# The context pass writes into the tiles of self attention, and three loads and stores are cut or moved

## The reference

```python
x = x + tanh(g_xattn[0]) * router_attention(layernorm(x), f, f, ctx, Wq, Wk, Wv, Wlq, Wlk, Wo, bo)
x = x + tanh(g_ffn[0])   * quantised_ffn(layernorm(x), w1, conv_w, conv_b, w2)
x = x + tanh(g_xattn[1]) * attention(layernorm(x), ctx, ctx, Wq, bq, Wk, bk, Wv, bv, Wo, bo)
x = x + tanh(g_ffn[1])   * recurrence(layernorm(x), wf, uf, bf, wi, ui, bi, wc, uc, bc, wo, uo, bo, in_c)
```

## Time and profile before

| | us |
|---|---|
| median of three runs | 2679.94 (2677.76 to 2680.05) |
| the profiled execution, its own time | 2680.58 |
| its span, first to last instruction | 2678.8 |
| PE busy | 2359.8 (88% of the span) |
| DVE, ACT, POOL busy | 1442.3, 1061.0, 603.7 |
| `ctx` ends, `att` starts (its first POOL instruction) | 113.6 |
| `att` ends, `ffn` starts | 1061.6 |
| `ffn` ends, `xat` starts | 1608.1 |
| `xat` ends, `rec` starts | 2020.9 |

### The profile page before, as it was taken

How to read it: one execution, slowest core, us unless ns; L and a number is a source line. 1 busy time by engine, 2 the same in 40 slices (tenths; PEclk the granted TensorE clock), 3 DMA queues, 4 the chain that set the end, 5 groups by cost and what they waited for, 6 DMA issues and landing times. The chain is left out here.

```text
span 2678.8 us, 40715 instructions
## 1 busy us (share of the span) xinstructions
PE 2359.8 (88%) x16307; PEld 1553.5 (58%) x16348; DVE 1442.3 (54%) x1746; ACT 1061.0 (40%) x1227; POOL 603.7 (23%) x204
## 2 busy tenths in 40 slices
PE   7359999999999986798999877999978999999989
PEld 6235555555555543344445425766656788888867
DVE  4345565665655554477677766787753222222235
ACT  3324444444544532344455543444432222222222
POOL 0004545554646544000000002233220000000000
PEclk9679999999999988899999997999988999999999
DMA  8711010110110011111111112222213000000036
GB/s 243 182 34 38 12 46 18 38 46 10 46 41 15 25 44 63 60 44 52 47 47 53 43 63 61 70 84 71 99 68 114 32 31 31 31 31 31 16 143 219
DMA packets 102030, 163.73 MB, mean 61 GB/s; under 512 B 17012, under 2 KB 39540, under 8 KB 99118
## 3 DMA queue, kind: packets, MB, share of 16 engines
q1 hardware_dynamic: 95934, 150.82, 17.5%
q10 hardware_dynamic: 6000, 11.54, 1.1%
HBM read 112.63 MB, written 49.71 MB: 61 GB/s over the span
## 5 line engine op out<-in xcount | busy, mean ns | idle before, releaser
L1047 DVE TENSOR_REDUCE att_mx<-att_sn 128x2 f32<-128x1024 f32 x256 | 313.7, 1226 | 170.4 <-PE att_sn L854 168.1
L959 ACT ACTIVATE att_num<-att_st 128x2048 f32<-128x2048 f32 x128 | 240.5, 1879 | 147.1 <-PE att_st L842 90.3
L766 POOL TENSOR_TENSOR att_es<-att_es,att_num 128x2048 f32<-128x2048 f32 x64 | 293.0, 4578 | 15.6 <-ACT att_num L959 9.4
L762 POOL TENSOR_TENSOR att_es<-att_num 128x2048 f32<-128x2048 f32 x32 | 146.0, 4561 | 388.9 <-PE att_pj L824 343.8
L2405 ACT ACTIVATE rec_ga<-rec_g,rec_bg 128x512 f32<-128x512 f32 x84 | 57.1, 687 | 307.8 <-PE rec_g L2306 307.8
L2306 PE MATMUL rec_g<-weights_a_h,row_weights_h 128*128 128x512 f32 x384 | 153.5, 400 | 13.6 <-ACT rec_ga L2405 11.1
L854 PE MATMUL att_sn<-att_kh,att_qh 32*128 32x512 f32 x512 | 128.5, 498 | 38.2 <-DVE att_mx L1047 38.2
L2306 PE MATMUL rec_g<-weights_a_l,row_weights_h 128*128 128x512 f32 x384 | 152.2, 396 | 0.0
L2306 PE MATMUL rec_g<-weights_a_h,row_weights_l 128*128 128x512 f32 x384 | 151.9, 396 | 0.0
L1360 PE MATMUL ffn_h<-ffn_xqt,ffn_w 128*128 128x512 bf16 x486 | 119.4, 389 | 28.1 <-DVE ffn_hs L1615 21.2
L1615 DVE TENSOR_TENSOR ffn_hs<-ffn_h,ffn_fb 128x1024 f32<-128x1024 f32 x64 | 78.1, 1220 | 118.6 <-PE ffn_h L1360 109.2
(11 more groups left out here) (383 smaller groups left out, 5690.1 us busy)
## 6 DMA issues: line engine op xcount, KB each, us to landing
rows<-in_x SPq DMA_DIRECT2D x16, 1024.0 KB, 5.4
rows<-x SPq DMA_DIRECT2D x16, 1024.0 KB, 5.2
rows_b<-in_fside_BxSxS SPq DMA_DIRECT2D x8, 1024.0 KB, 7.6
heads<-att_o SPq DMA_DIRECT2D x32, 256.0 KB, 2.3
weights_b_l<-heads SPq DMA_DIRECT2D x8, 1024.0 KB, 5.4
x<-ffn_xr SPq DMA_DIRECT2D x32, 256.0 KB, 2.0
xat_xr<-x SPq DMA_DIRECT2D x8, 1024.0 KB, 5.3
x<-xat_xr SPq DMA_DIRECT2D x8, 1024.0 KB, 4.3
```

The costliest lines, as they stand in the source:

```text
L762: pool.tensor_tensor(ES[:], E[0][:], E[1][:], ALU.add).then_inc(s_sum, 1)
L766: pool.tensor_tensor(ES[:], ES[:], E[k][:], ALU.add).then_inc(s_sum, 1)
L959: act.activation(E[k][:], st_ps[:], ACT.Exp, scale=SCALE).then_inc(s_exp, 1)
L1047: dve.tensor_reduce(MX[c % 2][:, m // 2, 2 * DH * (m % 2):2 * DH * (m % 2) + DH + 1:DH], sn_ps[:], AX, ALU.max, negate=True).then_inc(s_ma ...
```

## The change

1. Self attention's tiles are allocated around `ctx`: it gets `weights_a` (WA), `weights_b` (WB), the row tiles `rows` (XROW) and `rows_b` (FROW), and Wq, Wk, x, f. It keeps Wlq and Wlk in WA and WB, then Wv in WA, then the next pass's Wk in WB and Wq in WA. The stages of Wv, the next Wk and the next Wq are XROW, FROW and the tile of the masked `rq`. Batch 0 of x and f is loaded in `ctx` too, and the layer norm of x is done there. `att` starts with these at hand, loads only Wv and the routers, and makes Wv's halves after the task `("k", 1)` of `AHEAD`.
2. In `ctx` the order of PE's list is new (`v` behind all `e`, two `k` before `e 6`), the routines of ACT and DVE are hung on other entries, and the keys lie in the memory of RK. The keys are stored by one DMA with 2464 numbers per partition; the DRAM layout is (P, C, B, G), so that a load of keys in `xat` has rows of 77 numbers where it had rows of 154.
3. `ffn` loads the first matrix in four column parts, the heads of batch 1 after the first; the second matrix is loaded after the rows of batch 1. `hidden(0, 0)` waits for the first part alone, and `low_half(1)` comes behind `scaled(0, 1)`.
4. `xat`: nothing waits for the tables but the first `q`; the tanh is made after `AHEAD`, and its users wait there. The last batch's rows are stored tile by tile, 4 x 256 KB.

```diff
-    ORDER = [("rq", 0), ("rk", 0), ("rq", 1), ("rk", 1), ("v", 0), ("e", 0), ("e", 1),
...
-             ("rq", 4), ("rk", 4), ("v", 3), ("e", 6), ("e", 7), ("v", 4)] + [("k", i) for i in range(2 * C)]
+    ORDER = [("rq", 0), ("rk", 0), ("rq", 1), ("rk", 1), ("e", 0), ("rq", 2), ("rk", 2), ("e", 1), ("e", 2),
+             ("rq", 3), ("rk", 3), ("e", 3), ("rq", 4), ("rk", 4), ("e", 4), ("e", 5), ("k", 0), ("k", 1),
+             ("e", 6), ("e", 7)] + [("v", t) for t in range(NT)] + [("k", i) for i in range(2, 2 * C)]
...
+        NAMES = ("lq", "lk", "k", "v", "next_k", "next_q")
...
+        stage = {"lq": quarter(0), "lk": quarter(1), "k": quarter(2), "v": XROW[:], "next_k": FROW[:],
+                 "next_q": RQS[:, 0:C, :]}
...
+            for n, dram in (("lq", Wlq), ("lk", Wlk), ("k", Wk), ("v", Wv), ("next_k", next_wk)):
+                sp.dma_start(stage[n], kxn(dram)).then_inc(s_w[n], 16)
...
+            load_second(3)
+            for group, n in enumerate(("lq", "lk", "k")):
+                sp.wait_ge(s_lo, step(n))
+                load_second(group)
...
+            for b in range(5):
+                store_routers(b)
+            sp.wait_ge(s_lo, step("v"))
+            sp.dma_start(XROW[:], first(x)).then_inc(s_row, 16)
+            sp.wait_ge(s_lo, step("next_k"))
+            sp.dma_start(FROW[:], first(f)).then_inc(s_frow, 16)
+            for b in range(5, B):
+                store_routers(b)
+            sp.wait_ge(made["e"], B)
+            sp.dma_start(stage["next_q"], kxn(next_wq)).then_inc(s_w["next_q"], 16)
+            sp.wait_ge(s_sign, 4)
+            sp.dma_start(t1_s, TERNARY[0]).then_inc(s_store, 16)
+            for t in range(NT):
                 store_values(t)
...
-            for b in range(B):
-                sp.dma_start(k1_s[b].rearrange("p (c g) -> p c g", c=C), K[:, :, b * G:b * G + G]).then_inc(s_store, 16)
+            sp.wait_ge(taken["k"], 2 * C)
+            sp.dma_start(k1_s, RKS[:, 0:C * N]).then_inc(s_store, 16)
             sp.wait_ge(s_sign, 8)
             sp.dma_start(t2_s, TERNARY[1]).then_inc(s_store, 16)
...
-                if (kind, i) == ("v", 2):
+                if (kind, i) == ("rq", 3):
                     total(0)
-            total(1)
+                if (kind, i) == ("v", 4):
+                    total(1)
...
+            TODO = {("rq", 0): [("high", "k")], ("rk", 4): [("high", "v"), ("high", "next_k")],
+                    ("e", 4): [("sign", 0, 0)], ("e", 5): [("sign", 0, 1)], ("e", 7): [("sign", 0, 2), ("sign", 0, 3)],
+                    ("v", 4): [("high", "next_q")], ("k", 2): [("sign", 1, 0)], ("k", 3): [("sign", 1, 1)],
+                    ("k", 4): [("sign", 1, 2)], ("k", 5): [("sign", 1, 3)], ("k", 7): [("rows",)]}
...
+            TODO = {("rk", 0): lambda: low("k"), ("rk", 1): lambda: sums(0, 0), ("e", 0): lambda: sums(0, 1),
+                    ("rk", 2): lambda: sums(0, 2), ("e", 1): lambda: sums(0, 3), ("e", 2): lambda: mean(0),
+                    ("rk", 3): lambda: whole(0, 0), ("e", 3): lambda: whole(0, 1), ("rk", 4): lambda: low("v"),
+                    ("e", 4): lambda: low("next_k"), ("e", 5): lambda: whole(0, 2), ("e", 6): lambda: whole(0, 3),
+                    ("e", 7): lambda: sums(1, 0), ("v", 0): lambda: sums(1, 1), ("v", 1): lambda: sums(1, 2),
+                    ("v", 2): lambda: sums(1, 3), ("v", 3): lambda: mean(1)}
...
+            whole(1, 0)
+            low("next_q")
+            for j in range(1, 4):
                 whole(1, j)
-
+            next_rows()
...
-            load_x(0)
-            load_f(0)
-            w.load(sp)
+            sp.sem_inc(s_x, 16)
+            sp.sem_inc(s_f, 16)
             for c in range(C):
                 load_routers(0, c)
+            w.load(sp)
...
-            w.hi(act)
+            act.sem_inc(s_norm, T)
...
                 for task in AHEAD:
                     job(task)
+                    if task[:2] == ("k", 1):
+                        w.hi(act)
...
+                    if task[:2] == ("k", 1):
+                        w.lo(dve)
...
-            sp.dma_start(W1[:].rearrange("p k n -> p (k n)"), w1).then_inc(s_w1, 16)
-            sp.dma_start(W2[:].rearrange("p k n -> p (k n)"), w2).then_inc(s_w2, 16)
+            def load_first(group):
+                own = slice(HG * P * group, HG * P * group + HG * P)
+                sp.dma_start(W1[:, :, own], w1.rearrange("p (k n) -> p k n", k=C)[:, :, own]).then_inc(s_w1[group], 16)
+
+            load_first(0)
             sp.wait_ge(s_x1, T)
             sp.dma_start(f32(OL[:]), batch_rows(o_s, 1)).then_inc(s_o, 16)
+            for group in range(1, GROUPS):
+                load_first(group)
...
+                if not back:
+                    sp.dma_start(W2[:].rearrange("p k n -> p (k n)"), w2).then_inc(s_w2, 16)
...
-            pe.wait_ge(s_w1, 16)
+            hidden(0, 0)
             pe.wait_ge(s_dg, 2)
-            hidden(0, 0)
...
                 scaled(b, 1)
+                if not back:
+                    low_half(1)
...
-            low_half(1)
             scaled(0, 0)
...
-            store(B - 1)
-            sp.wait_ge(s_store, B * 16 + 1)
+            for t in range(T):
+                sp.wait_ge(taken["out"], (B - 1) * T + t + 1)
+                sp.dma_start(rows(x3_s, B - 1)[:, t, :], XR[:, t, :]).then_inc(s_store, 16)
+            sp.wait_ge(s_store, (B - 1 + T) * 16 + 1)
...
-            act.wait_ge(s_cols, 48)
-            act.activation(TG[:], TG[:], ACT.Tanh).then_inc(s_act0, 1)
+            def gates():
+                act.wait_ge(s_cols, 48)
+                act.activation(TG[:], TG[:], ACT.Tanh).then_inc(s_act0, 1)
...
                 for task in AHEAD:
                     job(-1, task)
+                gates()
```

More of the change, by code:

```diff
@@ L189, in context_pass @@
         TERNARY = [SW[i][:].bitcast(BF16)[:, 0:C * HID] for i in range(2)]
-        names = [("lq", Wlq), ("lk", Wlk), ("v", Wv), ("k", Wk)]
+        NAMES = ("lq", "lk", "k", "v", "next_k", "next_q")
+        ln = LayerNorm(ps, XROW, XROW)
+        shift = ps.sb("shift", [P, T])
+        s_row, s_rown, s_frow, s_rows, s_norm = (ps.sem(n) for n in ("row", "rown", "frow", "rows", "norm"))
         s_x, s_const, s_ident, s_masks = (ps.sem(n) for n in ("x", "const", "ident", "masks"))
-        s_w = [ps.sem(f"w{i}") for i in range(4)]
+        s_w = {n: ps.sem(f"w_{n}") for n in NAMES}
         s_hi, s_lo, s_xt, s_xhi, s_xlo = (ps.sem(n) for n in ("hi", "lo", "xt", "xhi", "xlo"))
@@ L232, in _, with load_second @@
                 sp.dma_start(SW[0][:, chunk(j)], w1[j * P:j * P + P, :]).then_inc(s_raw[0][j], 16)
-            for group in range(4):
-                sp.wait_ge(s_lo, group + 1)
+            def load_second(group):
                 for m in range(HG):
@@ L378, in _, with low @@
                     act.wait_ge(made["k"], i + 1)
+                    act.wait_ge(made["e"], 6 if i < 2 else B)
                     act.activation(K[:, c, HALF * half:HALF * half + HALF], src[:, 0:HALF], ACT.Identity,
                                    bias=BK[:, c:c + 1]).then_inc(taken["k"], 1)
-            signs(1)
+                for todo in TODO.get((kind, i), []):
+                    if todo[0] == "high":
+                        free_of(todo[1])
+                        high(todo[1])
+                    elif todo[0] == "sign":
+                        sign(*todo[1:])
+                    else:
+                        next_rows()
         @block.vector
         def _(dve):
-            def low(i):
-                n = names[i][0]
-                dve.wait_ge(s_hi, i + 1)
-                dve.tensor_tensor(W[n][1][:], stage(i), f32(W[n][0][:]), ALU.subtract).then_inc(s_lo, 1)
+            def low(n):
+                dve.wait_ge(s_hi, step(n))
+                dve.tensor_tensor(W[n][1][:], stage[n], f32(W[n][0][:]), ALU.subtract).then_inc(s_lo, 1)
             def sums(i, j):
@@ L447, in _ @@
                     TODO[kind, i]()
-            for j in range(4):
-                sums(1, j)
-            mean(1)
-            for j in range(4):
+            whole(1, 0)
+            low("next_q")
+            for j in range(1, 4):
                 whole(1, j)
+            next_rows()
 class LayerNorm:
@@ L1094, in ahead @@
                 dve.wait_ge(s_ones, 4)
-                for part in range(4):
-                    normalise(0, part)
                 for task in AHEAD:
@@ L1356, in hidden @@
                     pe.wait_ge(s_hs, b * PAIRS + pair)
+                if known(b, 1) and pair % 2 == 0:
+                    pe.wait_ge(s_w1[pair // 2], 16)
                 for m in range(2):
@@ L1941, in group @@
                     ln.pool_power(pool, B)
-            clock(pool, group, lambda: ln.pool_power(pool, 1), lambda: None)
+            clock(pool, group, ahead, lambda: None)
         @block.tensor
@@ L2037, in job @@
                 elif kind == "q":
-                    if not (isinstance(b, int) and b == 0):
```

(3 more changed lines are left out.)

137 lines of the change are left out of this document (71 added, 66 removed).

## The result

| | before | after |
|---|---|---|
| median, four runs of each on one chip | 2678.85 (2674.69 to 2680.05) | 2618.99 (2617.83 to 2623.53) |
| ratio | | 0.978, 95% interval 0.9766 to 0.9795 |
| the profiled execution, its span | 2680.58, 2678.8 | 2617.84, 2616.0 |
| length of `ctx` | 113.6 | 109.3 |
| `att` | 948.0 | 911.0 |

The changed kernel is 59.9 us faster where 51.3 was forecast: its time lies outside the forecast's 2624 to 2632, at the low edge of the range. PE's busy time is almost what it was the earlier trace rows; the gain is idle time.

The account below looks back on a forecast made before the run. PE bounds the kernel, busy 2359.8 of 2678.8 us, so only its idle time counts. 5.2 + 30.0 - 0.8 + 11.4 + 3.4 + 2.1 = 51.3 us gives a median of 2628.6 (forecast 2624 to 2632, range 2619 to 2640).

Parts of the forecast that it names:

- Start of `att`: At `att`'s start, loads and preparation ahead of PE go away, so PE starts 30.0 us earlier; bounds 29.5 to 30.5.
- Wv's halves: In `AHEAD` of `att`, making these delays DVE's maximum and costs PE 0.8 us; bounds nothing to 2.4.
- `ctx`, 5.2 us: Longer work but a shorter drain in `ctx`: `att` begins at 108.4, not 113.61; bounds gain 9.6 to loss 2.4.
- The first rival: Moved work comes out at `ctx`'s end through waits at `e 4` to `e 7`; `att` begins 113 to 119; chance 0.22.
- The drain: End of `ctx`: keys and ternary matrix, 3.36 MB, take 8.5 us plus 1.7 latency; SP's last wait some 10 us.
- `ffn`, 11.4 us: At `ffn`'s start, the second hidden pair starts at 1072.4 instead of 1083.80: 11.4 us; bounds 8 to 13.2.
- That bound (13.2: Upper bound for `ffn`'s start: with the clock up, the second pair takes 1.8 us instead of 3.59.
- `xat`, 5.5 us: In `xat`, ACT's first copy comes 3.4 us earlier and SP's last store wait is 2.1 us shorter.
- Key loads: In `xat`, loads with 256 runs of 77 numbers instead of 128 of 154 change nothing, both ways.
- the clock in `ffn`: Part of a rival: clock up early in `ffn`, with a shorter `ctx`, gives 2620 to 2623; chance 0.12.
- a lighter `e 7`: Same rival in `ctx`: DVE has no wait at `e 7`, signs end near 93; 2620 to 2623; chance 0.12.
- the loops' periods don't change: Inside the passes nothing touches the loops' periods; the prediction is wrong if they change.

Follow-up runs that it names:

- the join: Kernel before with points 1 and 2 of the change and the new key layout; alone against the kernel before: 2648.76 us, ratio 0.9898.
- keys_by_batch: Changed kernel with the old layout, load and store of the keys, in eight transfers batch by batch: 2642.12 us, ratio 0.9872 to the kernel before.
- low_half_first: Changed kernel with the low half of batch 1's heads ahead of the first scaling on DVE again: 2634.36 us, ratio 0.9835 to the kernel before.
- first_whole: Changed kernel with `ffn`'s first matrix in four parts issued together, the first pair waiting for all: 2631.14 us, ratio 0.9831 to the kernel before.
- the first set: The result's runs: the changed kernel beside the kernel before on one chip, median 2618.99 us against 2678.85.

## Why the prediction was right, and where it wasn't

The mechanism held in all passes, and over three chips the gain was 49 to 60 us around a forecast of 51.3. By its steps:

- *Start of `att`, 30.0 us.* PE started 2.3 us after the pass, as forecast. Wv's halves, 0.8 in the sum, cost 0.6: from PE's first scores for a maximum to the one that stood at 176.79 it takes 10.0 us in all ten profiles with the join and 9.5 in the four without, because PE waits 0.5 us for DVE's maximum behind the low half.

```profile
138.00 2.29 DVE L143 TENSOR_TENSOR att_wvl<-att_num,att_wvh 128x2048 fp32r<-128x2048 f32 x1
142.09 0.50 PE L909 MATMUL att_sn<-att_kh,att_qh 32*128 32x512 f32 x2 [0.50 <-DVE att_mx L1099]
```

  Together 29.2, and the profiles have 29.0. That it fits to 0.2 is luck: in single executions what follows this point in the pass varies by 10 us.
- *`ctx`, 5.2 us.* 3.7 measured, 4.3 in the first profile. There four terms were off and cancel down to 0.9 us. The store of router 5 landed 2.7 us late: x went out at 63.48 and not at 62.5, f behind a low half at 65.38, the store at 66.07; the work from there to the last sign took 24.5 us and not 25.9; and the ternary store left 1.2 us after its sign, since SP waits for the last two key copies first; and the drain below was shorter. The first rival (the moved work comes out at the end) was right about the place, `e 7`, but not about the size: the whole wait is worth 4.7 us, and most of it was in my sum already.
- *The drain.* 8.4 us of wait as against "some 10". The sum held nothing for what eight stores cost SP's queue; the new form doesn't pay it, so this didn't show. `keys_by_batch` shows it: 11 us for the old form, half of it in the queue.
- *`ffn`, 11.4 us.* Undersized: 14.8. The pair came 11.6 us earlier, as forecast, but I charged it at half clock. That bound (13.2, "if the clock is up") should have been the value: in the kernel before, PE waited 9.41 us ahead of the pair, in the forecast's own schedule 1.4. With a wait of 4.79 us ahead of it (`low_half_first`), or of 5.10 ahead of the first pair (`first_whole`), the pair again took 3.57 and 3.41 us. The other 1.5 us lie further on; they are not assigned to an edit.
- *`xat`, 5.5 us.* 4.8 measured. ACT's first copy comes 3.2 us earlier, and SP's last wait is 1.7 us as forecast. The Trainium skill, "DMA: Bandwidth & Descriptors", section "Anatomy of one DMA", gives its formula for DMAs issued from GpSimd, which the prediction didn't say; these stores go out from SP. The estimate by it was 1.8 us between the two waits, measured 2.1.
- *Key loads, nothing.* 0.1 us each, hidden. By the Trainium skill, the same page, section "Specifications", full rate needs transfers of 512 B and more. The stores of 308 B runs, which SP waits for, agree, with 119 GB/s; the loads were hidden at either length.
- *What nothing in the sum had:* `rec`, which isn't touched, is 1.6 us shorter in nearly every profile of a kernel with the join. I can't name the cause.

That the first result stayed at the edge of the range is luck as well. The range reached down to 2619 only because the clock in `ffn` and a lighter `e 7` were put there; the low times of the first set came from something else, the clock inside `att`. The prediction took "the loops' periods don't change" for "the pass's length doesn't change", and with the quads at the end of `att`, where PE waits for DVE again and again, 0.3 to 5.1 us at a time, that is only good to ±6 us (911.0 to 923.5 with the join).

## To carry to other kernels

At a seam, work out which engine is late after the edit, and count the waits that an early engine's queue puts in front of it: an issue on SP that had been beside other work (eight stores, 5.9 us) comes to stand on the path when the order changes. When PE is the late engine behind a wait of several us, take the first work behind it at full clock once that wait is gone (3.59 us became 1.89 here; the convolution behind it took 3.40 both times); when PE isn't late, its clock is worth nothing. Compare small edits by the length of their own pass over several executions, since the same program's untouched passes move by more than such an edit is worth.

## What was not expected of the hardware

- After the same wait of 1.60 us, in the same program on two chips, the clock fell to 0.50 in one execution and stayed at 1.00 in the other; the end of `att` took 164.2 and 174.5 us. No run here shows what decides it: with PE kept busy at the seams the clock still fell 36 us after the start of `att` and 52 us after that of `ffn`.
- Four loads of 512 KB in rows of 1 KB took 0.75 us of issue each, one of 2 MB 0.34.
- Eight stores with 512 runs of 308 B each kept the queue for 0.74 us apiece, and in the window behind the last issue 119 GB/s were moved at a DMA share of 1.39.
